# A fused decoder layer in fp16 pairs: two transposes of the second stage go to fp32, and low parts move from GpSimd to VectorE

## The reference, cut to what matters

```
x = _layernorm(x + _L0_attn_ref(x, ...))                 # linear + windowed attention, gated
x = _layernorm(x + _L0_xattn_ref(x, ctx_1024, ctx_1024, Wq, Wk, Wv, Wo))
x = _layernorm(x + _L0_ffn_ref(x, router, 32 experts, shared expert))
```

```
q = x @ Wq.T ; k = ctx @ Wk.T ; v = ctx @ Wv.T
attn = softmax(q k^T / sqrt(16)) ; out = (attn v) @ Wo.T
```

## Time and profile before

| | |
|---|---|
| median of 3 runs | 779.04 us (772.43 to 781.46) |
| profiled execution, its own time | 777.08 us |
| its span, first to last instruction | 775.3 us |
| granted TensorE clock, mean | 0.92 of full speed |
| busy share of the span | PE 78%, PEld 65%, DVE 66%, ACT 63%, POOL 67% |

### The profile page before, as it was taken

The page is one execution under the profiler, slowest core; times in us unless marked ns, Lnnn a source line. Parts: engine busy times, 40 slices in busy tenths (PEclk is TensorE's granted clock), DMA queues, the critical chain, the costliest instruction groups (busy, mean ns, idle before and its releaser), DMA issues.

```text
span 775.3 us, 24821 instructions
## 1 busy us (share of the span) xinstructions
PE 603.7 (78%) x8356; PEld 506.1 (65%) x8356; DVE 512.5 (66%) x2022; ACT 489.8 (63%) x1336; POOL 517.3 (67%) x667
## 2 busy tenths in 40 slices
PE   2899999999997567788678777863687777777384
PEld 1678989888886556676566566652676666666263
DVE  2988999988885234688878875671555455454365
ACT  3899999998996346777666666440455555455122
POOL 4758999999898624657877876683055555555574
PEclk9999999999998769998978998786999999999788
DMA  9310000001000022143453544355644354442194
GB/s 293 106 28 3 3 2 3 3 14 50 2 3 2 1 63 72 55 142 121 145 158 111 159 138 130 110 180 161 193 136 111 108 154 144 141 132 81 34 347 178
DMA packets 53643, 77.84 MB, mean 100 GB/s; under 512 B 8456, under 2 KB 42512, under 8 KB 52880
## 3 DMA queue, kind: packets, MB, share of 16 engines
q1 hardware_dynamic: 42768, 56.50, 25.0%
q0 software_dynamic: 7632, 16.87, 6.0%
q10 hardware_dynamic: 3120, 2.88, 1.1%
HBM read 48.62 MB, written 27.49 MB: 98 GB/s over the span
## 4 chain that ended last, share of the span: by engine, by line
PE 29%; issue 11%; POOL 10%; DVE 7%; ACT 6%; another core or an unknown queue 1%; DMA 1%; ACTq 0%; DVEq 0%; POOLq 0%; SPq 0%
PE bank L2298 6%; PE bank L1759 4%; PE bank L2269 3%; POOL x_rows L1392 3%; PE bank L2238 3%; POOL we_lo L1363 3%; PE bank L2287 2%; PE bank L1908 2%; ACT pT L1465 1%; PE bank L2279 1%; PE bank L1848 1%; ACT we_hi L1433 1%; DVE eh L2200 1%; PE bank L1807 1%
## 5 line engine op out<-in xcount | busy, mean ns | idle before, releaser
L2080 POOL DMA_INDIRECT y_rows<-front,ix x95 | 93.5, 985 | 106.6 <-DVE ix L2184 78.9
L565 ACT ACTIVATE sc<-sc,mn 128x128 f32<-128x128 f32 x256 | 82.6, 417 | 2.5 <-DVE mn L781 2.5
L2105 ACT ACTIVATE gT<-bank 128x512 f16<-128x512 f16 x95 | 56.4, 595 | 27.4 <-DVE eh_lo L2188 10.3
L1392 POOL DMA_INDIRECT x_rows<-rows,slot_ix x64 | 64.3, 1005 | 13.9 <-issue 13.9
L1363 POOL TENSOR_TENSOR we_lo<-east,we_hi 128x256 f16<-128x256 f32 (+1 forms) x80 | 59.6, 773 | 0.7
L781 DVE CUSTOM_DVE_ANT_0 sc<-bank,rel 128x128 f32<-128x128 f32 x256 | 57.6, 286 | 0.8 <-issue 0.5
L2180 DVE COPY front<-bank 128x256 f32<-128x256 f32 x63 | 26.4, 419 | 42.5 <-PE bank L2298 37.0
L1552 DVE TENSOR_REDUCE mnx<-bank 128x4 f32<-128x512 f32 x64 | 39.6, 720 | 14.4 <-PE bank L1807 14.4
L790 DVE TENSOR_TENSOR pT_lo<-bank,pT_hi 128x512 f16<-128x512 f32 x64 | 43.1, 675 | 5.2 <-ACT pT_hi L572 5.1
L965 PE MATMUL bank<-hT,w_hi 128*128 128x128 f16 x384 | 41.9, 222 | 1.2 <-POOL hT L375 0.9
L1465 ACT ACTIVATE pT<-bank 128x512 f32<-128x512 f32 x64 | 33.3, 599 | 14.9 <-PE bank L1833 14.7
(11 more groups left out here) (316 smaller groups left out, 2435.0 us busy)
## 6 DMA issues: line engine op xcount, KB each, us to landing
east<-in_experts SPq DMA_DIRECT2D x32, 384.0 KB, 3.4
hT<-x_rows SPq DMA_DIRECT2D x95, 129.0 KB
rows<-xhl SPq DMA_DIRECT2D x16, 512.0 KB
hT<-y_rows SPq DMA_DIRECT2D x16, 512.0 KB, 5.5
x_rows<-pad_block SPq DMA_DIRECT2D x32, 129.0 KB, 2.6
wst<-in_wcat SPq DMA_DIRECT2D x8, 256.0 KB, 7.2
front<-in_ctx_t SPq DMA_DIRECT2D x16, 128.0 KB
out<-fin ACTq DMA_DIRECT2D x16, 128.0 KB, 4.7
```

The costliest lines, as they stand in the source:

```text
L565: done = act.activation(sc[:, g, j], sc[:, g, j], ACT.Exp, bias=mn[:, n % 2, g, j:j + 1], scale=-1.0)
L1392: pool.indirect_dma_start(shared.x_rows, bass.IndirectOffsetOnAxis(ap=slot_ix[:, n, k:k + 1], axis=0), rows4[:, q, k], None).then_inc(shar ...
L2080: pool.indirect_dma_start(c.y_rows, bass.IndirectOffsetOnAxis(ap=ix[:, n % IX], axis=0), yo[:, n % YO], None, bounds_check=NDEST - 1, oob_ ...
L2105: act.activation(gT[:, n % U], GT_BANK[n % len(GT_BANK)], ACT.Copy).then_inc(gt_r, 1)
```

## The change

1. Query input and attention rows are no longer split before the transpose. PE transposes the fp32 rows (two transposes of 128x128 fp32 in place of four in fp16), ACT takes the high part out of PSUM (128x256 fp32 to fp16) and DVE the low part, from PSUM and the high part. `x1_high`, `x1_low`, `ao_high`, `ao_low` are gone; `x1T_high`, `x1T_low`, `aT_high`, `aT_low` replace `x1T_` and `aT_`.
2. `c_low` and `we_low` for k=1 (two pieces) move from POOL to DVE.
3. On PE `ao_T` stands ahead of `k_proj`, and `x1_T` ahead of `counts`. On ACT `aT_high` stands ahead of `xk_high`. On DVE `xq_low`, `aT_low`, `xk_low` stand ahead of `weights`, `x1T_low` behind it, `c_low` between `groups` and `x2`, `we_low` behind `chosen`.
4. Bank places: CN (counts) shares the bank of S0, LG and T0; XT2 shares that of S1 and T1; XT stays with TX and GU0.

```diff
-        ORDERS = [["S0", "LG", "T0"],
-                  ["S1", "CN", "T1"],
+        ORDERS = [["S0", "LG", "CN", "T0"],
+                  ["S1", "XT2", "T1"],
                   ["S2", "XPV", "T2"],
                   ["S3", "MT", "T3"],
-                  ["TX", "XT2", "XT", "GU0"],
+                  ["TX", "XT", "GU0"],
...
 # POOL
                 for i in range(NB + 10):
-                    x1_low(i)
                     scatter(i - 10, 2)
-                    we_low(i - 4, 0)
                     scatter(i - 10, 3)
-                    c_low(i - 1)
-                    ao_low(i - 4)
+                    we_low(i - 4)
                     pow_(i - 5)
                     xhl_low(i - 5)
                     scatter(i - 9, 0)
-                    we_low(i - 6, 1)
                     scatter(i - 9, 1)
...
 # ACT
-                def x1T_(n):
+                def x1T_high(n):
...
-                        act.activation(x1T[:, n % 2], flipped("XT"), ACT.Copy).then_inc(emptied["XT"], 1)
+                        act.activation(x1T[:, n % 2, 0], features("XT"), ACT.Copy).then_inc(x1hi_r, 1)
...
-                    x1_high(i)
...
                     logits_exp(i - 6)
+                    aT_high(i - 5)
                     xk_high(i - 2)
-                    aT_(i - 5)
-                    x1T_(i)
+                    x1T_high(i)
                     xv_(i - 3)
                     minT_(i - 3)
-                    ao_high(i - 4)
...
 # DVE
+                def x1T_low(n):
+                    if FRONT_X <= n < NB:
+                        dve.wait_ge(x1hi_r, n + 1)
+                        dve.tensor_tensor(x1T[:, n % 2, 1], features("XT"), x1T[:, n % 2, 0], ALU.subtract).then_inc(emptied["XT"], 1)
+
+                def aT_low(n):
+                    if live(n):
+                        dve.wait_ge(aThi_r, n + 1)
+                        dve.tensor_tensor(aT[:, n % 2, 1], features("XT2"), aT[:, n % 2, 0], ALU.subtract).then_inc(emptied["XT2"], 1)
...
                     min_parts(i - 3)
+                    xq_low(i - 2)
+                    aT_low(i - 5)
+                    xk_low(i - 2)
                     weights(i - 7)
-                    xq_low(i - 2)
-                    xk_low(i - 2)
+                    x1T_low(i)
                     places(i - 7)
...
                     groups(i - 6)
+                    c_low(i - 1)
                     x2(i - 5)
...
                     chosen(i - 6)
+                    we_low(i - 6)
                     sh_add(i - FIRST_SH - 1)
...
 # PE
                     if FRONT_X <= n < NB:
                         wait_turn(pe, "XT", n)
-                        pe.wait_ge(x1lo_r, n + 1)
-                        flip("XT", x1[:, n % 2])
+                        for k in range(KT):
+                            last = pe.transpose(features("XT")[:, k], xs[:, n, k * P:(k + 1) * P], ident[:])
+                        last.then_inc(filled["XT"], 1)
...
                     logits(i - 6)
+                    ao_T(i - 5)
                     k_proj(i - 2)
-                    ao_T(i - 5)
                     heads_back(i - 4)
+                    x1_T(i)
                     counts(i - 7)
-                    x1_T(i)
                     v_proj(i - 3)
```

More of the change, by code:

```diff
@@ L1345, in _, with we_low @@
                     pool.memset(t, v).then_inc(ones_set, 1)
[L1347 to L1359, removed]
+                def we_low(n):
                     if live(n):
+                        k = 0
                         for j, piece in enumerate(PIECES[k]):
@@ L1471, in oT_, with aT_high @@
                         act.activation(oT[:], room["OT"][:], ACT.Copy).then_inc(emptied["OT"], 1)
-                def ao_high(n):
-                    if live(n):
-                        act.wait_ge(xpv_rd, n + 1)
-                        wait(act, filled["XT2"], n - 1)
-                        act.activation(aox[:, n % 2, 0], ao[:, n % 2], ACT.Copy).then_inc(aohi_r, 1)
-                def aT_(n):
+                def aT_high(n):
                     if live(n):
@@ L1482, in aT_ @@
                         wait(act, filled["XWO"], n - 1)
-                        act.activation(aT[:, n % 2], flipped("XT2"), ACT.Copy).then_inc(emptied["XT2"], 1)
+                        act.activation(aT[:, n % 2, 0], features("XT2"), ACT.Copy).then_inc(aThi_r, 1)
                 def xhl_high(n):
@@ L1575, in xq_low, with c_low, we_low @@
                                                  ).then_inc(emptied["XPQ"], 1)
+                def x1T_low(n):
[6 more added lines that the diff above has]
+                        dve.tensor_tensor(aT[:, n % 2, 1], features("XT2"), aT[:, n % 2, 0], ALU.subtract).then_inc(emptied["XT2"], 1)
+                def c_low(n):
+                    if FRONT <= n < NB:
+                        dve.wait_ge(chi_r, n + 1)
+                        wait(dve, filled["XPK"], n - 1)
+                        wait(dve, filled["XPV"], n - 1)
+                        dve.tensor_tensor(c_lo[:, n % 2], cst[:, n % 2], c_hi[:, n % 2], ALU.subtract).then_inc(clo_r, 1)
+                def we_low(n):
+                    if live(n):
+                        k = 1
+                        for j, piece in enumerate(PIECES[k]):
+                            dve.wait_ge(we_hi_done[k], len(PIECES[k]) * n + j + 1)
+                            dve.tensor_tensor(pair(shared.we_lo, piece, n), arrived(piece), pair(shared.we_hi, piece, n), ALU.subtract
+                                              ).then_inc(we_lo_done[k], 1)
                 def rsx_(n):
@@ L1585, in ao_ @@
                         dve.wait_ge(xpv_rec, n + 1)
-                        wait(dve, aolo_r, n - 1)
+                        wait(dve, filled["XT2"], n - 1)
                         dve.tensor_tensor(ao[:, n % 2].rearrange("p (h d) -> p h d", h=NH), o_heads[:, :, 0:HD],
@@ L1862, in ao_T @@
                         wait_turn(pe, "XT2", n)
-                        pe.wait_ge(aolo_r, n + 1)
-                        flip("XT2", aox[:, n % 2])
+                        pe.wait_ge(xpv_rd, n + 1)
+                        for k in range(KT):
+                            last = pe.transpose(features("XT2")[:, k], ao[:, n % 2, k * P:(k + 1) * P], ident[:])
+                        last.then_inc(filled["XT2"], 1)
                 def out_proj(n):
```

23 lines of the change are left out of this document (9 added, 14 removed).

## The result

The kernel after takes 823.32 us (median of 4 runs, 808.54 to 832.05) against 777.01 for the kernel before: 1.0484 times, 95% interval 1.031 to 1.0658. I had predicted 782.0 and a range up to 792. Two of the four runs (826.04 and 832.05 us) count as slow and the ratio leaves them out: by the mean of the other two, 814.57, the loss is 38 us, by the median of all four 46. The profiled execution is one of 820.6 us.

A forecast was written before the change was run, and what follows sets the result against it. The prediction took a loop of DVE and POOL, with ACT's copies, as the bound; its terms summed to +2.9 us on the profiled 777.08, 780.0, and with 1.96 for the median 782.0; range 768 to 792.

The forecast's parts named there:

- the price of POOL's subtractions: POOL per iteration: losing three subtractions of 0.66 and the weight group, 1.79, cuts its work from 11.35 to about 7.6 us.
- it is padding and scatters together that starve PE: Stage end: PE's starving ends with the scatters, which finish 3.6 us earlier; -3.0 us, bounds 0 and -10.
- about 7: Stage end: PE's unexplained waits during the padding would fall from 10.1 to about 7 us.
- The pair of iterations: Middle of the stage, i=11 to 16: a pair goes from 28.24 to 29.08 us, +0.84; three pairs, +2.5.
- a changed clock: PE in the stage: a change of its granted clock would upset the early terms, sums of PE stretches; no size given.
- DVE's added work: DVE per iteration: five added instructions cost 2.02 us, 4.04 for a pair.
- The stalls: DVE beside POOL: old stalls of 3.7 us per pair shrink by 1.2, new weight pieces add 0.6.
- Rival (a): i=7 to 17: DVE becomes the bound, its stalls moved but not relieved; +12 us, 794; chance 0.20.
- (b): Rival for the loop: POOL's load paced it, stalls go to almost nothing, a pair takes 26.0; -12, 770 us; chance 0.15.
- (c): Rival for the stage end: PE's starving depends on overlap by a threshold and vanishes; 7 us more gained, 775; chance 0.15.
- i=3 to 10: Early iterations: i=4 to 6 gain 2.1 us on PE; i=7, 8 and 9 lose 0.9, 0.5 and 1.8.
- The late iterations and the end: i=18 to 20 lose 1.9 us by bank waits and aT_low's order; the end gains 3.4 as scatters finish earlier.

The follow-up runs named there:

- a_same: Kernel after, unchanged, measured again with its own profile beside the kernel before: 1.0547 times, 815.38 us as mean of its two lower runs against 780.67.
- spread_2: Repeat of the kernel after with only POOL's list reordered, at most two scatters together: 793.78 us, against 833.56 for the kernel after and 779.22 before.
- a_spread: Kernel after with only POOL's list reordered so that at most two scatters stand together: 790.09 us, 1.0135 times the kernel before.
- b_same: Kernel before, unchanged, with a second profile of its own: fill_row at 519.02 us, against 518.14 in the first profile.
- a_we1: Kernel after with the second weight group back on POOL, at most two scatters together: 0.9922 times the kernel before, where that takes 722 us.
- we1_2: Repeat of the kernel after with the second weight group back on POOL: 781.31 us, against 779.22 for the kernel before.
- b_we1: Kernel before with only the second group of weight pieces moved to DVE, leaving three scatters together with one subtraction among them: 1.0240 times the kernel before.
- w1_gap: Kernel after, second weight group back on POOL, scatter 0 between the power and xhl_low: fill_row at 515.89 us, against 506.74 for a_we1; cost 0.4%.
- E: Theory that aT_low stands too early in DVE's list, tested by moving it later in w1_gap's kernel: i=18 to fill_row 58.4 us, against 58.2.
- b_train: Kernel before with only POOL's list reordered so that four scatters stand back to back: 1.0006 times the kernel before in its first run.
- b_train3: Third run of the kernel before with four scatters back to back, beside a kernel before at 779 us: 1.0314 times.
- b_train2: Second run of the kernel before with four scatters back to back, beside a kernel before at 722 us: 1.0011 times.

## Why the prediction was wrong

The step of the prediction that failed is the price of POOL's subtractions: I priced them only as load. "POOL loses three subtractions of 0.66 and the weight group of two" was for me pure relief, and the scatters' order did not occur in the sum. I had read that the scatters run back to back at the stage's end, 1.27 us apart, and that PE then waits 10.1 us for nothing that the profile shows. From that I drew the wrong sentence: "it is padding and scatters together that starve PE". The kernel after has the counterexample. There a run of scatters lasts until 555.40 and the padding starts only at 562.50. PE's unexplained waits (all of them from 536 to 585 us) begin at 549 and are over at 557.40:

```profile
PE bank L1910 <- issue: 6.7, 7, 1.9
```

```profile
557.40 0.28 PE L1910 MATMUL bank<-hT,w_hi 128*128 128x128 f16 x1 [0.45 <-issue]
...
562.50 14.08 SPq L1308 DMA_DIRECT2D x_rows<-pad_block  x16
```

So it takes no padding: the scatters do it alone (three waits of under 0.5 us lie behind their end), and the one group of padding without scatters that ran at full speed said so too. The total of 6.7 us is near the "about 7" that I had forecast for the waits during the padding, but that is luck: they lie ahead of the padding, and the stage's end gained nothing. Had I asked what else in the trace happens during a scatter, the late signals stood in the kernel before (28 of 82 over 0.5 us), and the diff shows that it takes every subtraction among the four scatters away. What the runs showed in place of "pure relief": 25 to 40 us for the order of POOL's list alone.

Point by point:
- **The pair of iterations**: forecast 29.08, measured 36.97 (28.99 and 36.50 in one trace of a_same). Without the train (spread_2, i=12 to 18) a pair takes 28.3, and 27.6 in a_spread, from 28.2 in b_same. So apart from the train the size of this term was about right, a little too dear. The prediction had named a changed clock as a thing that would upset its early terms; it did not upset these, but it fell from i=11 on.
- **DVE's added work**: right in price. Groups of the kernel after, 380 to 455 us:

```profile
L1565 DVE TENSOR_TENSOR we_lo<-east,we_hi 128x512 f16<-128x512 f32 x5 | 3.4, 684 | 0.0
...
L1551 DVE TENSOR_TENSOR aT<-bank,aT 128x256 f16<-128x256 f32 x4 | 1.7, 424 | 2.8 <-ACT aT L1451 2.8
L1558 DVE TENSOR_TENSOR front<-front 128x256 f16<-128x256 f32 x4 | 1.7, 425 | 0.1
...
L1654 DVE SCALAR_TENSOR_TENSOR wt<-wraw,winv 128x64 f32<-128x64 f32 x2 | 0.5, 225 | 0.1
```

  0.42 to 0.43 and 0.68, as taken from the earlier trace rows; `c_low` (L1558) is not at the 0.65 of L843. POOL is mostly idle in this kernel, so no run here tests the rule of sharing of the Trainium skill (GPSIMD Engine Reference, section "Key points") on it.
- **The stalls**: too small a relief. The product that had taken 1.13 takes 0.22. In a_spread DVE is busy 69.7 us over six iterations, in b_same 65.9: 0.6 more for each, where 2.02 of work were added. I had let a third of the stalls go; 1.4 of my 1.85 per iteration went.
- **Rival (a), 794**: its time came close to that of a_spread (790.1) and spread_2 (793.8), but for another reason than its own. Its stalls were not there. Rivals (b), 770, and (c), 775, are tested by no run: a_we1's 0.9922 has the weight group back on POOL and ran at 722, and the kernel after was never run there.
- **i=3 to 10**: forecast +1.1, measured -0.1. i=4 to 6 gave -3.1 (forecast -2.1); all of it came in i=4 and 5, and i=6, for which 0.9 had been forecast and from whose rows that price was read, gave nothing. i=7 to 9 gave +3.0 together (forecast +3.2). DVE's wait for the power fell to 0.78 in i=12 (forecast 1.00).
- **The late iterations and the end**: forecast +1.9 up to fill_row and -3.4 for the end, of which 3.0 behind fill_row. Measured +13 from i=18 to fill_row in all three profiles of the kernel after (66.9 to 67.4, from 54.1 to 54.6), and +0.7 behind it. a_spread has +10 of the 13 (64.8) without full trains, we1_2 only +2 (56.3). The 8 us between these two are the weight group on DVE and scatter 0 ahead of `xhl_low`. The group alone in the kernel before (b_we1) makes it 59.3, 4.7 more than b_same, which is about its own 4.4 us of work; the scatter's place alone (w1_gap against a_we1, 58.2 and 55.5, in the other condition) makes 2.7. This sums to 7.4 of the 8 us, an estimate across two conditions; E, another try, fell.

## What to carry to other kernels

Before taking work from an engine, look at what it stood between. Here instructions that issue indirect DMAs held up the signals of another engine when they stood together, and the work between them was what kept the kernel fast in one of its two conditions. If the chain names an unknown releaser, or an engine waits for one whose instruction has long ended, compare the time of the signal with the instruction's end, and ask what every other engine does in the gap. Read the granted clock of the same stretch beside it. And measure an order that gained or lost in both conditions, if the kernel before shows two: b_train was 1.0006 and 1.0011 in one and 1.0314 in the other.

## What the runs showed of the hardware that was not expected

- PE's completion signals came up to 4.7 us late while GpSimd issued indirect DMAs back to back (5.0 when paired in order), and at most 0.09 us late outside them (a few of 0.1 to 0.9 in other traces). ACT's signals in the same trains were at most 0.6 late, but for one of 2.1 in b_train3 and one of 0.7 in b_we1.
- The lateness comes and goes with the chip or the launch, not with the kernel: median 1.91 us in b_train3 (chip 0) and 0.01 in b_train2 (chip 8), same program. In the second condition PE's unexplained waits at the stage's end are gone too: in b_same 9.9 us in 9 times, in b_train2 none. A few single signals of up to 5.1 us stay there (4 of 108 over 0.5 in b_train, all behind 552 us, in the third stage).
- Two iterations with the same trains took 28.99 us at a granted clock of 0.88 and 36.50 at 0.73, within one trace (a_same); in a_spread, without full trains, two take 27.6.
- The third stage, in which POOL scatters `y_rows` with 95 indirect DMAs, shows the same two conditions: from fill_row to the end 257 to 264 us in one, 203 to 208 in the other (kernels without filler). That this is the same cause is likely, not shown. What sets the condition is open; the scatters themselves mostly take 0.96 to 1.1 us in both.
